# One list table's 34 products on TensorE, moved from behind a step's row products to half ahead of them and half behind

## What is computed

```python
def _L0_gnn_ref(x, indices, values, bias):
    row, col = (indices[0], indices[1])
    gathered = values[:, None] * x[col]
    out = jax.ops.segment_sum(gathered, row, num_segments=OUT_FEATURES)
    return out + bias
...
xn = _layernorm(x, axis=-1)
x = x + _L0_gnn_ref(xn, edge_index, edge_weight, node_vec1) + _L0_mix_ref(xn[None], ...)[0]
x = x + _L0_ffn_ref(_layernorm(x, axis=-1)[None], ...)[0]
```

## Time and profile before

| | before |
|---|---|
| median of 3 runs | 2530.46 us (2526.78 to 2535.07) |
| profiled execution's own time | 2506.26 us |
| its span, first to last instruction | 2504.5 us |
| TensorE busy | 2195.2 us (88%) |
| VectorE busy | 1781.8 us (71%) |
| GpSimd busy | 1465.3 us (59%) |
| ScalarE busy | 1280.1 us (51%) |
| mean granted TensorE clock | 0.932 |

### The profile page before, as it was taken

One profiled execution on the slowest core, in us unless ns is written; L12 is line 12 of the kernel. 1 busy time (PEld: TensorE's weight loads), 2 busy tenths in 40 slices (PEclk: granted clock), 3 DMA queues, 4 the chain that ended last, 5 costly groups with the idle time before them and its releaser, 6 DMA issues. The chain is left out here.

```text
span 2504.5 us, 46512 instructions
## 1 busy us (share of the span) xinstructions
PE 2195.2 (88%) x16549; PEld 1900.3 (76%) x16550; DVE 1781.8 (71%) x3160; ACT 1280.1 (51%) x2683; POOL 1465.3 (59%) x1342
## 2 busy tenths in 40 slices
PE   7987899898998899989999999998889945999993
PEld 4656678777877788777877778777777744999993
DVE  7989977777776777776777777777656657555552
ACT  2225445554554455545555455545433345888872
POOL 4760366666666666666656666566655503788883
PEclk9998899999999999999999999999999967999997
DMA  5542422232222222322222222222334453555555
GB/s 144 146 129 76 144 80 78 77 92 80 80 76 89 78 80 76 89 81 80 83 85 81 84 82 85 76 83 79 94 106 135 140 187 52 81 82 82 83 83 132
DMA packets 160939, 235.96 MB, mean 94 GB/s; under 512 B 54834, under 2 KB 121805, under 8 KB 160490
## 3 DMA queue, kind: packets, MB, share of 16 engines
q0 software_dynamic: 70896, 164.43, 26.1%
q1 hardware_dynamic: 75536, 55.29, 8.1%
q10 hardware_dynamic: 14314, 13.68, 1.6%
HBM read 186.46 MB, written 53.24 MB: 96 GB/s over the span
## 5 line engine op out<-in xcount | busy, mean ns | idle before, releaser
L834 POOL DMA_INDIRECT picked<-xn_dram,place x1029 | 1058.9, 1029 | 771.8 <-PE bank L932 328.6
L1054 ACT COPY stage<-bank 128x512 f32<-128x512 f32 x343 | 200.7, 585 | 741.6 <-remote 567.7
L932 PE MATMUL bank<-picked,pick_w 128*128 128x256 f32 x2058 | 512.0, 383 | 8.7 <-issue 8.2
L932 PEld LDWEIGHTS bank<-picked,pick_w 128*128 128x128 f32 x2058 | 397.8, 194 | 71.7 <-issue 16.1
L928 PE MATMUL bank<-window,stage 128*128 128x256 f32 x1568 | 415.0, 408 | 12.8 <-issue 8.6
L928 PEld LDWEIGHTS bank<-window,stage 128*128 128x128 f32 x1568 | 300.3, 202 | 58.9 <-issue 18.7
L920 PE MATMUL bank<-hot_w,hots 128*128 128x128 bf16 x4116 | 314.7, 228 | 29.5 <-issue 27.0
L1060 ACT ACTIVATE pick_w<-hots,weights 128x128 f32<-128x128 bf16 x1029 | 338.6, 397 | 0.0
L1369 DVE TENSOR_TENSOR hot_w<-hots,bank 128x1536 bf16<-128x1536 bf16 x343 | 327.1, 954 | 11.9
L920 PEld LDWEIGHTS bank<-hot_w,hots 128*128 128x128 bf16 x4116 | 272.4, 103 | 69.6 <-issue 36.8
L1201 DVE TENSOR_TENSOR vals<-hot_t,field_rep 128x1666 bf16<-128x1666 bf16 x150 | 156.4, 1043 | 217.0 <-remote 198.7
(11 more groups left out here) (262 smaller groups left out, 3430.4 us busy)
## 6 DMA issues: line engine op xcount, KB each, us to landing
picked<-xn_dram,place POOLq DMA_INDIRECT x1029
w<-in_L_ffn_W_dram SPq DMA_DIRECT2D x16, 512.0 KB, 8.6
xn_dram<-xn ACTq DMA_DIRECT2D x49, 128.0 KB, 2.0
xT_dram<-xT ACTq DMA_DIRECT2D x49, 128.0 KB, 2.2
base_dram<-acc SPq DMA_DIRECT2D x7, 896.0 KB
sum_dram<-acc SPq DMA_DIRECT2D x7, 896.0 KB
z_dram<-vals SPq DMA_DIRECT2D x7, 896.0 KB
out_dram<-sum_dram SPq DMA_DIRECT2D x1, 6250.0 KB, 22.3
```

The costliest lines, as they stand in the source:

```text
L834: pool.indirect_dma_start(out=picked[:, i % SETS * PICK + q, :], out_offset=None, in_=xn_dram, in_offset=bass.IndirectOffsetOnAxis(ap=plac ...
L932: mm = pe.matmul(sum_ps[pp], pick_w[i % SETS][:, q, :], picked[:, i % SETS * PICK + q, :], start=False, stop=(q == PICK - 1))
L1054: act.copy(block_sb[pp].rearrange("p j c -> p (j c)"), banks[pp][:, :]).then_inc(a_copied, 1)
```

## The change

`make_table(s)` is cut into `begin_table(s)`, which has the three waits and the first 17 products, and `end_table(s)`, with the other 17 and the semaphore. In a unit's last step `begin_table` is called ahead of `rows` and `end_table` behind it. Outside the units, `make_table` calls both one after the other.

```diff
-            def make_table(s):
+            def begin_table(s):
                 pe.wait_ge(vals_done, 3 * s + 3)
                 pe.wait_ge(slot_done, s + 1)
                 if later(s):
                     pe.wait_ge(unpacked, s)
-                for c in range(CH):
-                    mm = pe.matmul(table_ps, slot[:, c, :], vals[:, c, :, :], start=(c == 0), stop=(c == CH - 1))
+                for c in range(CH // 2):
+                    pe.matmul(table_ps, slot[:, c, :], vals[:, c, :, :], start=(c == 0), stop=False)
+
+            def end_table(s):
+                for c in range(CH // 2, CH):
+                    mm = pe.matmul(table_ps, slot[:, c, :], vals[:, c, :, :], start=False, stop=(c == CH - 1))
                 mm.then_inc(table_made, 1)
+
+            def make_table(s):
+                begin_table(s)
+                end_table(s)
...
                         blocks(t + i + 1, (i + 1) % 4, (odd + i + 1) % 2)
                     elif after:
                         blocks(t + BU, 0, 1 - odd)
+                    if more and i == 6:
+                        begin_table(s)
                     rows(t + i, i, g * GRP + k, (odd + i) % 2, par)
...
                     if more and i == 6:
-                        make_table(s)
+                        end_table(s)
```

## The result

The changed kernel takes 2597.93 us (median, 2596.08 to 2602.11), the kernel before 2529.36 us on the same chip (2526.78 to 2535.07). The ratio is 1.027, with a 95% interval of 1.026 to 1.029. I had forecast 2485 us and a range up to 2575: the sign is wrong and the time lies outside the range.

What follows compares the result with a forecast made beforehand. TensorE was taken to set the pace, with halts and a lowered clock on top. A shorter stall (-50 us) and slot waits (+5) summed to -45 us, giving 2485 us against the runs' median; range 2400 to 2575.

Steps and rivals of the forecast that it cites:

- What bounds the kernel: TensorE sets the pace in the 42 units: 35.14 us each, 29.65 if it never stops; the rest is halts and clock.
- The moved products: 17 table products go ahead of the last rows, 1.13 us per unit; sum on TensorE 0.
- The changes between fp32 and bf16: Two more switches of number format on TensorE per unit: taken as no cost, upper bound 18 us.
- The slots: The table's three waits, now ahead of the last rows, may hold TensorE: 0 to 21 us, taken as 5 us.
- The later rows: The last step's `o_done` comes 1.13 us later, covered by other engines' idling: taken as 0, up to 47 us.
- The stall: TensorE's halts in the base shorten as fewer products are open: 24 to 127 us gained, taken as 50 us.
- The clock: TensorE's granted clock in the units stays at 0.94: taken as 0, between 60 us gained and 45 us lost.
- Slower: Rival: the stall moves ahead of the last rows and is paid twice, 2594 us or 2550; chance 0.24.
- The stall goes altogether: Rival: 29 short products start no stall and the base alone drains in time, 2403 down to 2343 us; chance 0.18.
- Nothing changes: Rival: the number of products between GpSimd's pauses sets the stall, not their order; 2530 us, within 7; chance 0.22.
- the rule of the Trainium skill: TensorE's queue holds 64 instructions, so 29 products with loads (58) fit: would give the full -127 us instead of -50.

Runs made afterwards that it cites:

- run with the copy moved: Changed kernel with ScalarE's copy of the base moved from the unit's step 0 to step 1, behind the evacuation of step 2's blocks: 2557.74 us, ratio 1.017 to 1.024.
- run with two pauses: Kernel before with GpSimd waiting for the table ahead of step 2's gathers and for the base ahead of step 3's: 2520.50 us, ratio 0.994.
- run with no longer one: Changed kernel with the base's halves behind the rows of steps 0 and 1, its copy and ranking one step later: 2531.94 us, ratio 1.009.

## Why the prediction was wrong

**What bounds the kernel** was read right. Without gathers a unit takes 29.4 to 29.5 us, and the 5.6 us above it are gaps and clock, both of which go with the gathers.

**The moved products** cost nothing: the two kernels without gathers are 1.2 us apart. The changes between fp32 and bf16, bounded by 18 us, cost nothing that shows.

**The slots.** I took 5 us. TensorE's list for the changed kernel has no wait for `slot` at line 871. It is 0.

**The later rows.** I took 0, since `values` idled 5.18 us for the table. That wait went to nearly nothing, and the cover with it; the changed kernel has VectorE wait elsewhere, for the base. GpSimd's 426.2 us of waits for `o_done` (282.2 before) were taken to be covered by the four sets. Its last sign, 6.5 us behind a late release, follows the halt and didn't start it.

**The stall, -50 us: this step failed.** It came out as +52 us of "issue" waits from the one profile to the other (127.0 to 178.9), and as 9 us of waits for ScalarE's copy of the blocks. Its first half was right: with 17 products ahead of the rows, the table is reported in time. What failed is the sentence by which the base, once the table no longer fills the queue, "may issue 17 more before the halt". I treated the base as the place where a stall started by the table is paid. It is itself a row as long, 34 and 12. That it was spared before because the table had taken the stall, and with it GpSimd's pause, just ahead of it, is my reading. Once the table passes, the base meets a GpSimd in full run, and ScalarE waits 8.3 us for its report in each of 42 units. The new place is dearer for two reasons: ScalarE's and VectorE's next steps hang on the base (0.5 to 0.7% by the run with the copy moved), and TensorE's halt there lasts longer (gaps of 5.96 us in the turn shown, 3.35 us in that of the earlier trace rows).

**The clock, 0: this step failed too**, as a consequence. I took it as unchanged because the base "stays". The gaps grew by 1.43 us a unit, the clock fell from 0.94 to 0.91, and the products took 0.93 us a unit longer: 39 us.

Together -50 + 5 + 0 became +60 for gaps and +39 for the clock, the 99 us between the two profiles' stretches; between the medians it is +68.6 us, as said above.

**The rivals.** "Slower" had the sign and, at 2594 us, nearly the time, but that was luck, as it hadn't the mechanism: the stall isn't paid twice and isn't ahead of the rows. It moved behind them. "The stall goes altogether" rested on the base being drained in time; its own counterargument, that the base with blocks is as long a row as the table with blocks, was the right sentence, and I gave it a half-line and no price. "Nothing changes" had the right cause, GpSimd's pauses, and the wrong conclusion. By the rule of the Trainium skill (TensorE: Matmul & The Clock Gate, section "Architectural detail: the array is 16× 32×32, not 1× 128×128") a queue holds 64 instructions; the trace after agrees as before, since TensorE halts after 31 products of the base, with their loads 62 instructions. It says when TensorE halts, not why the reports are late, and only the second was at stake.

**What is shown and what isn't.** Shown: the reports are late only with the gathers there; an unbroken row of them makes them late and a pause lets them through, with bytes and products unchanged; the change moves the late row from the table to the base. Argued only: that short products matter because they bring more reports per microsecond, and the run with two pauses, which halts in ordinary steps, speaks against their being needed. The row of 29 in the run with no longer one was late, the row of 29 at the table in the changed kernel was not, and I can't say what tells them apart. What in the chip holds a report back is open as well, GpSimd's issuing or its gathers' transfers, and so is why three steps ahead help and four don't.

## What to carry to other kernels

When a stall is found in one row of instructions, ask which row is next to meet the same condition if this one passes, and price that one; here it was the row behind, and it was dearer. When an engine halts for nothing that the profile shows and its consumers are released together, look at what every other engine is doing in that time, and remove that in one run before the stalled engine's order is tuned: one run without gathers would have given 278 us as the prize and the order as worth nothing. When an engine issues indirect gathers as here, try to hold it to the lead that it needs, not to the buffers that it has; here that was worth three times the change, and a step too many gave nothing.

## What the runs showed of the hardware

- With GpSimd issuing indirect gathers of 128 rows one after another (0.95 us each, 0.30 us between), ScalarE saw TensorE's semaphore some 7 us after the last product (base issued from 1200.94 to 1203.30, copy at 1210.40). With a pause of 2.39 us around it, the base of the same row of 46 was reported 1.13 us after its first product.
- TensorE issued 31 products of the base with their loads, 62 instructions, behind `rows` before it halted (the first at 1200.94, the 32nd at 1203.06). With two gathers of three the blocks' report was 3 us late in the turn shown, and it didn't halt.
- The cost isn't in proportion to the gathers: one or two of three left the kernel at 2227 and 2251 us, three at 2509, where GpSimd has no time left in a step.
- The same 1029 gathers, with GpSimd at most three steps ahead, cost by my estimate some 120 us more than none (0.937 of 2509 against 2230); at four steps ahead, 1.026 of 2509, some 345 us.
